# Splitting the late mixing weights, moving one plain copy to GpSimd and one small load to SyncE's queue

## The reference

```python
w1 = jax.lax.complex(w1r, w1i)
w2 = jax.lax.complex(w2r, w2i)
x_ft = _sht(x)
top = jnp.einsum('bixy,ioxy->boxy', x_ft[:, :, :M1, :M2], w1)
bot = jnp.einsum('bixy,ioxy->boxy', x_ft[:, :, -M1:, :M2], w2)
...
return _isht(out_ft)
```

## Time and profile before

| what | value |
|---|---|
| median of 3 runs | 1313.02 us |
| the profiled execution: its time | 1314.89 us |
| its span in the trace | 1313.1 us |
| TensorE matmul busy | 993.3 us (76%) |
| VectorE busy | 859.5 us (65%) |
| ScalarE busy | 654.5 us (50%) |
| GpSimd busy | 565.4 us (43%) |
| moved by DMA | 93.12 MB, mean 71 GB/s |

### The profile page before, as it was taken

The page is one execution under the profiler, slowest core; times in us unless marked ns, Lnnn a source line. Parts: engine busy times, 40 slices in busy tenths (PEclk is TensorE's granted clock), DMA queues, the critical chain, the costliest instruction groups (busy, mean ns, idle before and its releaser), DMA issues. The chain is left out here.

```text
span 1313.1 us, 23822 instructions
## 1 busy us (share of the span) xinstructions
PE 993.3 (76%) x6645; PEld 837.2 (64%) x6646; DVE 859.5 (65%) x2743; ACT 654.5 (50%) x1400; POOL 565.4 (43%) x731
## 2 busy tenths in 40 slices
PE   9948654876666775768676344089999999999997
PEld 7838653654545654656565233078888888888886
DVE  7716533675578898897984753256666676666665
ACT  3428641445859768676855421134444444444443
POOL 3310000110231566656664667535555555555554
PEclk9979876987778878787787555589999999999999
DMA  9996947780011010000000001111111111111110
GB/s 269 221 247 137 255 108 191 191 185 20 20 38 32 20 44 24 26 16 24 19 17 27 22 22 35 34 43 45 43 46 49 40 49 47 45 49 49 46 38 2
DMA packets 103604, 93.12 MB, mean 71 GB/s; under 512 B 7884, under 2 KB 92236, under 8 KB 102761
## 3 DMA queue, kind: packets, MB, share of 16 engines
q1 hardware_dynamic: 74905, 62.02, 19.6%
q0 software_dynamic: 9088, 17.33, 4.0%
q10 hardware_dynamic: 19536, 12.85, 3.8%
HBM read 55.61 MB, written 38.39 MB: 72 GB/s over the span
## 5 line engine op out<-in xcount | busy, mean ns | idle before, releaser
L1686 POOL DMA_INDIRECT out_dram<-res,index x156 | 156.0, 1000 | 218.0 <-DVE res L1769 190.0
L1816 ACT ACTIVATE sil<-ps_h 128x512 f32<-128x512 f32 x156 | 93.1, 597 | 255.0 <-PE ps_h L1868 255.0
L1734 DVE TENSOR_TENSOR act_rows<-ps_h,sil 128x512 f32<-128x512 f32 x156 | 107.9, 692 | 132.9 <-ACT sil L1816 132.9
L1887 PE MATMUL ps_y<-r_raw,aT 128*128 x1248 | 164.8, 275 | 0.0
L158 POOL DMA_INDIRECT slots<-x_sb,r_pos x128 | 130.9, 1023 | 54.2 <-issue 33.2
L1887 PEld LDWEIGHTS ps_y<-r_raw,aT 128*128 128x128 f32 x1248 | 151.6, 192 | 0.1
L1866 PE MATMUL ps_h<-wp,uTh 128*128 x312 | 137.6, 441 | 1.6 <-DVE uTl L1728 1.6
L1867 PE MATMUL ps_h<-wp,uTh 128*128 x312 | 124.7, 400 | 0.0
L1868 PE MATMUL ps_h<-wp,uTl 128*128 x312 | 123.1, 395 | 0.0
L1057 PE MATMUL ps_q<-wqkv,zT 128*128 128x256 f32 x256 | 114.2, 538 | 0.0
L1169 POOL TENSOR_TENSOR x_sb<-x_sb,sy 128x256 f32<-128x256 f32 x64 | 43.8, 684 | 138.0 <-ACT sy L1305 137.8
(11 more groups left out here) (242 smaller groups left out, 2465.4 us busy)
## 6 DMA issues: line engine op xcount, KB each, us to landing
slots<-zero SPq DMA_DIRECT2D x4, 2652.0 KB, 23.2
pay<-slots SPq DMA_DIRECT2D x39, 272.0 KB, 2.8
wc<-in_L_conv_w1r SPq DMA_DIRECT2D x4, 1024.0 KB, 15.1
wc<-in_L_conv_w1i SPq DMA_DIRECT2D x4, 1024.0 KB, 20.3
wc<-in_L_conv_w2r SPq DMA_DIRECT2D x4, 1024.0 KB, 21.7
wc<-in_L_conv_w2i SPq DMA_DIRECT2D x4, 1024.0 KB, 22.3
coefc<-coefficients ACTq DMA_DIRECT2D x16, 256.0 KB, 6.6
mixed<-mo ACTq DMA_DIRECT2D x16, 256.0 KB, 7.1
```

The costliest lines, as they stand in the source:

```text
L1686: nc.gpsimd.indirect_dma_start(out_rows, bass.IndirectOffsetOnAxis(at, 0), res[:, m % RES, :], None, bounds_check=TOKENS - 1, oob_is_err=F ...
L1734: nc.vector.tensor_tensor(act_rows[:, k], ps_h[:, k, :, DFF:], sil[:, k], ALU.mult).then_inc(s_act, 1)
L1816: nc.scalar.activation(sil[:, k], ps_h[:, k, :, 0:DFF], ACT.Silu).then_inc(s_sil, 1)
L1887: ins = nc.tensor.matmul(dst, aT[:, k, (2 * e + h) * P:(2 * e + h + 1) * P], raw[:, 4 + h, col], start=(h == 0), stop=(h == 1))
```

## The change

- The weights of steps 4 to 7 are loaded by `load_late` in pieces of one step (4 DMAs of 512 KB, rows of 512 bytes) instead of chunks of two steps (4 DMAs of 1 MB, rows of 1024 bytes). Each piece has a semaphore of its own and is requested when the step that used the same half slot is done: step 4's after step 0, 5's after 1, 6's after 2, 7's after 3.
- The plain copy of 32x512 in the upper blocks is made by GpSimd (4 for each step, 32 in all) with a new semaphore `s_sp`; TensorE and `load_coef` wait for it as well.
- `lw` is loaded first on SyncE's queue in block C instead of on ScalarE's.

```diff
+        def load_late(eng, n):
+            k = n % (WS * LW // LQ)
+            at = n * LQ % LW
+            for g in range(4):
+                eng.dma_start(wc[32 * g:32 * g + 32, k * LQ // LW, :, at:at + LQ, :].rearrange("i o l m -> i o (l m)"), w_late[g][n])\
+                    .then_inc(s_wq[k], 16)
...
                 def _(sp):
-                    for c in range(WS, L2 // LW):
-                        sp.wait_ge(s_mm, (c - WS + 1) * (LW // LQ))
-                        load_w(sp, c)
+                    for n in range(WS * LW // LQ, NCH):
+                        sp.wait_ge(s_mm, n - WS * LW // LQ + 1)
+                        load_late(sp, n)
...
                 def _(pool):
                     nc.gpsimd.memset(sblk[:, 1], 0.0).then_inc(s_zero, 1)
+                    pool.wait_ge(s_zero, 2)
+                    for n in range(NCH):
+                        k = n % 2
+                        pool.wait_ge(s_cc[k], n // 2 * 32 + 32)
+                        need(pool, s_mm, n - 1)
+                        for l in range(LQ):
+                            dst = sblk[64:96, k, l, :, RB:2 * RB].rearrange("p (q m) f -> p q m f", q=M // MQ)
+                            ins = nc.gpsimd.tensor_copy(dst, coefc[64:96, k, :, l])
+                            if l % 2:
+                                ins.then_inc(s_sp, 1)
...
                         need(act, s_sa, 2 * (n - 1))
+                        need(act, s_sp, 2 * (n - 1))
...
-                            nc.scalar.activation(dst[0:32], src, ACT.Copy)
                             nc.scalar.activation(dst[32:64, :, :, 0:B], src[:, :, :, B:RB], ACT.Copy, scale=-1.0)
...
                     for n in range(NCH):
-                        c = n * LQ // LW
-                        pe.wait_ge(s_w[c % WS], c // WS * 64 + 64)
+                        if n < WS * LW // LQ:
+                            pe.wait_ge(s_w[n * LQ // LW], 64)
+                        else:
+                            pe.wait_ge(s_wq[n - WS * LW // LQ], 64)
                         pe.wait_ge(s_sd, 2 * n + 1)
                         pe.wait_ge(s_sa, 2 * n + 1)
+                        pe.wait_ge(s_sp, 2 * n + 1)
...
             def _(sp):
+                sp.dma_start(lw[:, :, :], t["L1_conv_lin_w"].rearrange("i d c -> d i c")).then_inc(s_load, 16)
                 sp.dma_start(psyn[:, :, :], t["legendre_synthesis"].rearrange("p (m q) -> p m q", m=M)).then_inc(s_psyn, 16)
...
             def _(act):
-                act.dma_start(lw[:, :, :], t["L1_conv_lin_w"].rearrange("i d c -> d i c")).then_inc(s_load, 16)
```

More of the change, by code:

```diff
@@ L213, in spectral_conv @@
         s_w = [sem(f"mix_weights_{k}") for k in range(WS)]
+        s_wq = [sem(f"mix_weights_late_{k}") for k in range(WS * LW // LQ)]
+        w_late = [w.rearrange("i o (k l) m -> k i o (l m)", l=LQ) for w in spectral_w]
         w_view = [w.rearrange("i o (k l) m -> k i o (l m)", l=LW) for w in spectral_w]
@@ L403, in spectral_conv @@
             s_sa = sem("m_upper_blocks")
+            s_sp = sem("m_upper_plain_rows")
             s_mh = sem("m_first_degrees_mixed")
@@ L535, in _ @@
                         pe.wait_ge(s_sa, 2 * n + 2)
+                        pe.wait_ge(s_sp, 2 * n + 2)
                         need(pe, s_ea, n)
```

## The result

The change takes 1298.26 us (median of 4 runs, 1292.8 to 1300.93), the kernel before on the same chip 1315.09 (4 runs): a ratio of 0.9866, 95% interval 0.9826 to 0.9907. It is faster by 1.3%. The profiled execution took 1295.85 us for a span of 1294.0.

The account below looks back on a forecast made before the run. Late-weight transfer was taken to bound block B, and VectorE's wait for lw to hold block C; savings of 6.8 + 7.3 = 14.1 us from 1313.0 gave 1298.9 us, with 8 in 10 between 1290 and 1314.

Parts of the forecast that it names:

- Any change of duration behind block C: Sign of being wrong: the work after block C, which no edit touches, changes in length; no size given.
- What bounds block B: Block B ends by the transfer of 8.39 MB of late weights, 53.9 us from first request to landing at 171.22 us.
- The last landing: Block B: step 7's weights land at 171.2 us, from 110.1 + 0.6 + 48.4 + 12.1.
- 48.4 us: Block B: transfer time of all late weights in 512-byte rows at 173 GB/s, with 7.9 ns fixed cost a row.
- The last step: Block B: step 7 after a pause, TensorE first at half clock, takes 9.8 us to ScalarE's evacuation at 181.0 us.
- the VectorE limit: Block B: full exclusion by GpSimd copies of T us each ends step 7 at 155.7 + 32T, 181.3 for T = 0.8.
- GpSimd's relief of ScalarE "worth 0 at the end": Block B: moving the copy frees ScalarE 2.5 us a step, worth 0 unless the transfer were no longer the limit.
- lw: Block C: early lw leaves gin as next wait; first synthesis matmul at 209.4 instead of 216.7 us, 7.3 us saved.
- VectorE as bound: Rival, block B: full exclusion with GpSimd copies of 1.15 us, end at 192.5 us, kernel at 1310 us; chance 0.17.
- rows by the piece: Rival, block B: a weight row costs the same whatever its length, step 7 ends at 221.4, kernel 1339 us; chance 0.10.
- lw worth little: Rival, block C: gin was near behind lw, 4.3 us or less saved, kernel at 1302 to 1306 us; chance 0.08.
- Rows free and a small T: Rival, block B: short rows cost nothing, GpSimd's copy time T small; end at 177.0, kernel 1294.6 us; chance 0.10.

## Why the prediction was right

The time was forecast at 1298.9 us and measured at 1298.26; by the ratio, 1.34% faster against 1.07%. That the two times lie 0.6 us apart is luck: the forecast saved 14.1 us from 1313.0, while the kernel before measured 1315.1 beside the change and 16.8 were saved, 16.6 of them in blocks B and C of the profiled executions. The mechanisms were right in both blocks, and the forecast was short by 3.1 us in block B and long by 0.6 in block C. "Any change of duration behind block C" was to be a sign of being wrong; it changed by 2 us, but with a spread of 11 us there this sign could tell nothing.

- **What bounds block B.** Right: the transfer of the late weights, before and after. The change at the old request times lost 8.7 of the 9.9 us.
- **The last landing.** 171.2 forecast, 170.3 measured, from terms that were each a little off. The first request came at 111.0, not 110.7. The row's fixed cost was taken as 7.9 ns, which gave 173 GB/s; 175 to 182 were measured with late weights alone, so it is 3.3 to 6.9 ns here by the same working, and the term "48.4 us" should have been 46.1 to 47.9. The Trainium skill's sentence on 512 bytes (DMA: Bandwidth & Descriptors, Specifications), by which, as I read it, these rows should have kept the 189 GB/s of the longer ones, is borne out but for these 4 to 7%; at 256 bytes, below it, the rate fell to 156 to 161 GB/s. The rest of the 59.3 us, 11 to 13, stands against the 12.1 for coefficients and stores.
- **The last step: the mis-sized term.** "One step after a pause, TensorE at half clock for its first part ... 9.8 us." It took 7.41, evacuation at 177.77 instead of 181.0. The late piece was step 6's, landed at 158.7, and it was step 6 that ran cold (9.87), while step 7 had only 1.68 us of pause ahead of it. I had the pieces land 14 us apart (a quarter of my own two terms is 15.1), which with a step of 7.6 us between them is a pause of some 6 us; they landed 11.5 apart, and step 6 filled 9.87 of these. This is 2.4 of the 3.1 us by which block B beat its forecast of 6.8. Of the rest, 0.4 us are the landing, counted from the block's start, and 0.3 the VectorE limit that I had put just above. That the clock is the cause is shown by the run with the pause filled.
- **VectorE beside GpSimd.** GpSimd's copy took 0.67 us where I took 0.8. The full sum, "155.7 + 32T", would give 177.1 us with that, and it assumed that VectorE stands for all of GpSimd's copies. It waits for one instruction at a time, and block B with GpSimd's work doubled took 92.3 us and not 100 or more. That limit lay below the weights, not beside them; that both were put at 181 was chance. The Trainium skill's exclusion rule (SBUF — State Buffer, Who interferes with whom) holds, in turns: VectorE's 284 ns instruction took 609 at most in the change.
- **GpSimd's relief of ScalarE "worth 0 at the end".** Right alone (ratio 1.0008), not quite in the change: 2.4 us, by the clock of step 7. The condition that I gave, "unless the transfer were no longer the limit", missed this second way.
- **lw.** 7.3 us forecast, 6.7 in the change and 5.1 alone. lw landed in 3.1 us, the next wait was gin's, as said: the first matmul came 14.9 us behind the block's first issue, by the forecast 15.1. So it came 7.5 us earlier than before, but from there the stage took 21.6 us where it had taken 20.8, and the forecast had put that at no change.
- **The rivals.** VectorE as bound, rows by the piece and "lw worth little" did not come. Rows free and a small T named 177.0 for the end of step 7, closer to the 177.77 than mine, but by two errors that cancel: a landing at 167.2 where 170.3 was measured, and a last step of 9.8 us where it took 7.41.

## What to carry to other kernels

When a block ends with a transfer that keeps the DMA engines busy from its first request, move that first request forward and let as little work as possible stand behind its last landing; here an engine's relief alone gave nothing, and finer pieces alone 1.3 us. When a load is moved earlier or to a second queue, look at the small loads and stores that then queue beside it, for they become the next wait. And see what the last step's pause does to TensorE's clock: here a pause of 3.7 us instead of 1.7 made the step behind it 2.85 us longer.

## What the runs showed that I had not expected

- Work that nobody needs shortened a block: 3.7 us of matmuls made twice ahead of the last landing left a pause of 0.31 us, and step 7 took 7.41 instead of 10.26 us.
- An issue of a 512 KB weight DMA on ScalarE's queue, with other DMAs under way, held ScalarE for up to 6.33 us and its work behind it; on GpSimd's queue the issues took 0.78 to 1.13 us, but ScalarE's issue of a pair of stores then took 5.13.
- A second queue raised the mean rate of the transfer from 231 to 243 GB/s only. What holds these weights at 175 to 189 GB/s, with 512 as with 1024 bytes in a row and in small or large packets, was not found.
